# Where the ends of the expert rows, the copies of the partial sums and the first expert's steps stand in the queues of a fused mixer and mixture-of-experts kernel

## The reference

```python
x = L0_attn_x
xn = _layernorm(x)
# mixer: projection to 2*1024, causal depthwise convolution (4 taps), silu,
# a scan over time with 64 states, gate, projection back to 512, layernorm
attn = _layernorm(W_out(y * silu(x_gate)) + xn, ln_gamma, ln_beta)
# experts: 8 of them, each takes the 1024 rows with its highest scores
scores = (tanh(xn @ gate_w.T) + 1) * 0.5
vals, idx = top_k(scores.T, 1024)
y = _layernorm(xn[idx], ln_gamma, ln_beta)
h = gelu(y @ fc1s[e].T + b1s[e])          # 512 -> 2048
o = (h @ fc2s[e].T + b2s[e]) * kept_w     # 2048 -> 512
ffn = xn.at[idx].add(o)
return x + attn + ffn
```

## Time and profile before

| | us |
|---|---|
| median of three runs | 2714.39 |
| time of the profiled execution | 2714.52 |
| span of the profiled execution | 2712.8 |
| TensorE (matmul) busy in it | 2643.2 |
| VectorE busy | 2061.1 |
| ScalarE busy | 1484.9 |
| GpSimd busy | 685.4 |
| mean granted share of TensorE's clock | 0.996 |

### The profile page before, as it was taken

How to read it: one execution, slowest core, us unless ns; L and a number is a source line. 1 busy time by engine, 2 the same in 40 slices (tenths; PEclk the granted TensorE clock), 3 DMA queues, 4 the chain that set the end, 5 groups by cost and what they waited for, 6 DMA issues and landing times.

```text
span 2712.8 us, 41479 instructions
## 1 busy us (share of the span) xinstructions
PE 2643.2 (97%) x11818; PEld 2137.0 (79%) x11820; DVE 2061.1 (76%) x3533; ACT 1484.9 (55%) x2569; POOL 685.4 (25%) x1002
## 2 busy tenths in 40 slices
PE   8999999999999999999999999999999999999997
PEld 4588888888887788888778777887878778788886
DVE  8778888888788888888865867877678676786654
ACT  5744455555555555665445555565555555555552
POOL 5422222222221222224330313122141121411102
PEclk9999999999999999999999999999999999999999
DMA  9633323222333333224442425234262342533413
GB/s 365 248 124 109 108 79 95 90 92 95 96 105 109 109 109 109 78 93 124 151 129 93 121 71 137 78 91 116 70 147 70 94 125 67 131 87 89 102 47 70
DMA packets 139517, 299.99 MB, mean 111 GB/s; under 512 B 26080, under 2 KB 26208, under 8 KB 135520
## 3 DMA queue, kind: packets, MB, share of 16 engines
q1 hardware_dynamic: 105696, 201.54, 22.4%
q0 software_dynamic: 33664, 96.75, 14.9%
HBM read 244.46 MB, written 53.77 MB: 110 GB/s over the span
## 4 chain that ended last, share of the span: by engine, by line
PE 86%; DVE 6%; issue 4%; ACT 2%; DMA 1%; POOL 0%; DVEq 0%; SPq 0%; ACTq 0%; POOLq 0%
PE ring L1546 8%; PE ring L1547 8%; PE ring L1548 8%; PE po L2451 7%; PE po L2453 7%; PE po L2452 7%; PE pb L2451 4%; PE pb L2453 4%; PE pb L2452 4%; PE po L1584 4%; PE po L1585 4%; PE po L1586 4%; PE pc L2453 2%; PE pc L2451 2%; PE pc L2452 2%
## 5 line engine op out<-in xcount | busy, mean ns | idle before, releaser
L2451 PE MATMUL po<-w2h,hid_h 128*128 128x512 f32 x1024 | 404.9, 395 | 18.2 <-DVE res L2310 12.9
L2452 PE MATMUL po<-w2l,hid_h 128*128 128x512 f32 x1024 | 400.3, 391 | 0.0
L1546 PE MATMUL ring<-xt_h,w_h 128*128 128x512 f32 x1024 | 400.1, 391 | 0.1
L1547 PE MATMUL ring<-xt_l,w_h 128*128 128x512 f32 x1024 | 398.5, 389 | 0.0
L1548 PE MATMUL ring<-xt_h,w_l 128*128 128x512 f32 x1024 | 398.4, 389 | 0.0
L1339 DVE SCALAR_TENSOR_TENSOR u<-xin,cw,u 128x512 f32<-128x512 f32 x384 | 288.5, 751 | 74.2 <-issue 32.8
L2451 PEld LDWEIGHTS po<-w2h,hid_h 128*128 128x128 f32 x1024 | 193.4, 189 | 62.9 <-DVE res L2310 14.2
L1961 POOL DMA_INDIRECT out_dram<-res,idx_c x64 | 114.6, 1791 | 504.9 <-DVE res L2310 492.4
L1546 PEld LDWEIGHTS ring<-xt_h,w_h 128*128 128x128 f32 x1024 | 192.2, 188 | 41.0 <-DVE xt_l L542 0.9
L2452 PEld LDWEIGHTS po<-w2l,hid_h 128*128 128x128 f32 x1024 | 193.4, 189 | 38.7
L1548 PEld LDWEIGHTS ring<-xt_h,w_l 128*128 128x128 f32 x1024 | 192.2, 188 | 40.1
(11 more groups left out here) (294 smaller groups left out, 6255.5 us busy)
## 6 DMA issues: line engine op xcount, KB each, us to landing
w2r<-fc_in SPq DMA_DIRECT2D x256, 256.0 KB
wo<-wo_halves POOLq DMA_DIRECT2D x120, 512.0 KB, 4.2
w1r<-fc_in SPq DMA_DIRECT2D x144, 256.0 KB
x_tail<-x_in SPq DMA_DIRECT2D x64, 256.0 KB, 2.7
out_dram<-res SPq DMA_DIRECT2D x64, 256.0 KB, 2.0
g_x<-x_in SPq DMA_DIRECT2D x15, 1024.0 KB, 8.5
xt_rows<-g_xnt SPq DMA_DIRECT2D x15, 1024.0 KB, 10.2
rows<-xt_rows SPq DMA_DIRECT2D x15, 1024.0 KB, 6.2
```

The lines of the kernel that those rows point to most:

```text
L1546: pe.matmul(ring[r % 2][:, :], w_h[:, r, q], xt_h[:, k, :], start=(k == 0), stop=False)
L1547: pe.matmul(ring[r % 2][:, :], w_h[:, r, q], xt_l[:, k, :], start=False, stop=False)
L2451: pe.matmul(dst, ah, bh, start=start, stop=False, skip_group_check=more)
L2452: pe.matmul(dst, ah, bl, start=False, stop=False, skip_group_check=more)
```

## The change

It moves instructions and waits; no arithmetic is added but one ScalarE activation of a single column.

- **Row ends.** `rows_out` becomes `row_out`, one bank at a time. In the last pair (q = 7) the four row ends of the first half stand between the low parts of tiles 18 to 21 and of weights 16 and 17, and the first steps on the next expert's transposed rows (`T_HIGH_AT[0]`, `T_LOW_AT[0]`) stand there too.
- **Partial sums.** In every pair ScalarE copies `top` out of R0 before the gelu of `first`, not behind it.
- **Passage.** The gate activation 7 of the mixer's last block stands ahead of the second `y_high` copy; ScalarE's four `sum_rows` of that block move into the first four steps of expert 0; a one-column gelu stands ahead of the expert's first; VectorE makes the low part of the second weights later than the first weights'; each gelu waits for one bank's `take` and not for all four.
- **Expert 0.** GpSimd gathers expert 0's second rows first, then adds the mixer's beta, then gathers expert 1's first rows, and then takes the square roots for expert 0's second rows. The steps of VectorE, ScalarE and TensorE on rows stand at other step numbers (`ROWS_1_AT`, `ROWS_2_AT`, `TAIL_AT`, `BIAS_AT`, `T_AT`, `FIRST_..._AT`).
- **The end.** In expert 7 the last three tiles are shared bank by bank, not the last two.

```diff
--- before.py
+++ after.py
@@ -1280,10 +1280,13 @@
                 w_high(3)
             in_g(b, 6)
             side(1)
+            if last:
+                in_g(b, 7)
             y_high(b, 2)
             if first_turn:
                 w_high(4)
-            in_g(b, 7)
+            if not last:
+                in_g(b, 7)
             side(2)
             y_high(b, 3)
             side(3)
@@ -1301,11 +1304,8 @@
                 if last and k >= 2:
                     sums.first_high(act, k - 2)
                 ends.normal_rows(act, b, k)
-                if last and k >= 1:
-                    ends.sum_rows(act, b, k - 1)
             if last:
                 group_high(KD - 1)
-                ends.sum_rows(act, b, J - 1)
 
         act.wait_ge(sums.c_small_in, 16 * 8 + 1)
...
@@ -1721,7 +1721,7 @@
 LOWS = ("B11", "T1", "B22", "T3", "B21", "T2", "T4")
 BANKS = ("B11", "B12", "B22", "B21")
 P1, P2, P6, P5, P7, P4, P3 = range(1, 8)
...
@@ -1734,7 +1734,9 @@
 
 
     G = 2 * E
-    T_AT = (8, 9, 11, 12)
+    T_AT = (9, 10, 12, 13)
...
@@ -1972,16 +1978,15 @@
 
         pool.wait_ge(sums.c_t, KD + 1)
         pool.wait_ge(sums.c_in_all, NB * NW + 1)
+        take(idx_c[1][:, :], 1, 1)
+        pool.wait_ge(c_kp, 1 + 1)
+        gather(rows[1], idx_c[1], lambda j: c_ga[1])
         for j in range(J):
             ends.add_beta(pool, NB - 1, j)
         ends.inverse_std(pool, NB - 1)
-        take(idx_c[1][:, :], 1, 1)
-        pool.wait_ge(c_kp, 1 + 1)
-        gather(rows[1], idx_c[1], lambda j: c_ga[j])
+        next_rows(1, 0, 2)
         inverse_std(1)
-        gather_gates(ew.row_gates, idx_c[1], lambda j: c_ga[j])
-        pool.wait_ge(c_kp, 2 + 1)
-        next_rows(1, 0, 2)
+        gather_gates(ew.row_gates, idx_c[1], lambda j: c_ga[3])
         inverse_std(2)
         pool.wait_ge(c_t, 2 * KD + 1)
         next_rows(1, 1, 3)
...
@@ -2035,10 +2042,14 @@
         w_high(act, s, s)
 
     def first_low(dve, s):
-        if s == 1:
+        if s == 0:
+            w1_low(dve, 0)
+        else:
             dve.wait_ge(c_bias, 16 + 1)
             bias(dve, 0, 1)
-        w_low(dve, s, s)
+            w2_low_of(dve, 0)
+            w1_low(dve, 1)
+            w2_low_of(dve, 1)
 
...
@@ -2119,12 +2130,12 @@
             w2_high(e, 2 * q)
             if q < PAIRS - 1:
                 a_high(e, q + 1, here + P2)
+            act.wait_ge(c_p1, here + P6 + 1)
+            act.wait_ge(c_p2, shared(e, FT + 2 * q) - 128 + 1)
+            act.copy(top, R0[:, :]).then_inc(c_ge, 1)
             act.wait_ge(c_b1, e + 1 + 1)
             act.wait_ge(c_add, adds(e, q, ADD_FIRST) + 1)
             gelu(first, first, 2 * q).then_inc(c_ge, 1)
-            act.wait_ge(c_p1, here + P6 + 1)
-            act.wait_ge(c_p2, shared(e, FT + 2 * q) - 128 + 1)
-            act.copy(top, R0[:, :]).then_inc(c_ge, 1)
             act.wait_ge(c_ge, steps(e, q, TOP_LEFT) + 1)
             hid_high(e, 2 * q, first)
...
             if q == PAIRS - 1:
-                for x in (2, 3, 4, 5):
-                    store_high(e, x)
-                for x in (FT, FT + 1):
-                    w2_high(e, x)
+                store_high(e, 2)
+                w2_high(e, FT)
+                store_high(e, 3)
+                w2_high(e, FT + 1)
+                store_high(e, 4)
+                if not last:
+                    for k, name in T_HIGH_AT[0]:
+                        t_high(e + 1, k, name, here + P3)
+                store_high(e, 5)
...
-        act.wait_ge(ends.c_po, NB * J + 1)
+        act.wait_ge(c_b1, 1 + 1)
+        act.activation(warm, ends.half[:, 0:1], ACT.Gelu_apprx_tanh)
         for n in range(2 * FT):
             g, s = n // FT, n % FT
             raw_l = old_w(n)
+            if n < J:
+                act.wait_ge(ends.c_po, (NB - 1) * J + n + 1 + 1)
             act.wait_ge(c_p2, shared(0, n - 4) + 1 if n >= 4 else 1)
             if n >= 12:
                 act.wait_ge(ends.c_fin, NB * J + 1)
@@ -2186,6 +2205,8 @@
             act.copy(old_h(n)[:, :], raw_l).then_inc(c_hh, 1)
             if n + 2 < 2 * FT:
                 next_high(n + 2)
+            if n < J:
+                ends.sum_rows(act, NB - 1, n)
             if g == 0 and s - 1 in T_AT:
                 row_high(T_AT.index(s - 1))
             if g == 1:
...
+            elif s in TAIL_AT:
+                ends.scale(dve, NB - 1, TAIL_AT.index(s))
+                ends.finish(dve, NB - 1, TAIL_AT.index(s))
...
@@ -2302,13 +2323,12 @@
             dve.wait_ge(c_sc[j], 16 * g)
             dve.tensor_scalar(res[j][:, :], b2[:, :], kept[i][:, j, bass.ds(e, 1)], None, ALU.mult).then_inc(c_bw, 1)
 
-        def rows_out(e, i):
+        def row_out(e, i, j, count=2):
             g = 2 * e + i
             dve.wait_ge(c_bw, (g + 1) * J + 1)
-            for j in range(J):
-                dve.wait_ge(c_p2, 128 * e + J * (i * FT + FT - 2) + 2 * (j + 1) + 1)
-                dve.scalar_tensor_tensor(out=res[j][:, :], in0=po[j][:, :], scalar=kept[i][:, j, bass.ds(e, 1)],
-                                         in1=res[j][:, :], op0=ALU.mult, op1=ALU.add).then_inc(c_rw, 1)
+            dve.wait_ge(c_p2, 128 * e + J * (i * FT + FT - count) + count * (j + 1) + 1)
+            dve.scalar_tensor_tensor(out=res[j][:, :], in0=po[j][:, :], scalar=kept[i][:, j, bass.ds(e, 1)],
+                                     in1=res[j][:, :], op0=ALU.mult, op1=ALU.add).then_inc(c_rw, 1)
 
         def pair(e, q, last):
             first, low, top = hid_w[2 * q % 4], store_w[2 * q + 1], store_w[2 * q]
...
             if q == PAIRS - 1:
-                for x in (2, 3, 4, 5):
-                    hid_low(e, FT + x)
-                for x in (FT, FT + 1):
-                    w2_low(e, x)
+                hid_low(e, FT + 2)
+                w2_low(e, FT)
+                row_out(e, 0, 0)
+                hid_low(e, FT + 3)
+                w2_low(e, FT + 1)
+                row_out(e, 0, 1)
+                hid_low(e, FT + 4)
+                if not last:
+                    for step in T_LOW_AT[0]:
+                        t_step(e + 1, step, here + P3)
+                row_out(e, 0, 2)
+                hid_low(e, FT + 5)
+                row_out(e, 0, 3)
 
...
-            if g == 0 and 3 <= s < 3 + J:
-                ew.statistics(dve, 1, s - 3, rows[1])
-            if g == 0 and s >= FT - J:
-                row_statistics(1, 0, s - FT + J)
+            if g == 0 and s in ROWS_1_AT:
+                row_statistics(0, 1, ROWS_1_AT.index(s))
+            if g == 0 and s in ROWS_2_AT:
+                row_statistics(1, 0, ROWS_2_AT.index(s))
             if g == 1 and s < J:
                 row_statistics(1, 1, s)
             if n + 2 < 2 * FT:
-                w_low(dve, n + 2, n + 2)
+                w1_low(dve, n + 2)
+                w2_low_of(dve, n + 2)
             if g == 0:
                 tail(s)
-            if g == 0 and 3 <= s < 3 + J:
-                ew.normalise(dve, 1, s - 3, rows[1])
-            if g == 0 and s >= FT - J:
-                row_normalise(1, 0, s - FT + J)
+            if g == 0 and s in ROWS_1_AT:
+                row_normalise(0, 1, ROWS_1_AT.index(s))
+            if g == 0 and s in ROWS_2_AT:
+                row_normalise(1, 0, ROWS_2_AT.index(s))
...
@@ -2434,7 +2464,8 @@
                     w1_low_c(1, 0)
                     w1_low_b(1, 0)
             if n == FT - 1:
-                rows_out(0, 0)
+                for j in range(J):
...
@@ -2497,12 +2529,13 @@
             three(po[j][:, :], h[:, w], l[:, w], w2h[x % 4][:, :], w2l[x % 4][:, :], start, stop).then_inc(c_p2, 1)
 
         def old_share(n):
+            pe.wait_ge(c_wl, 2 * n + 2 + 1)
             pe.wait_ge(c_hl, n + 1 + 1)
             if n == 0:
                 pe.wait_ge(ends.c_po, NB * J + 1)
-            if n == FT:
-                pe.wait_ge(c_rw, J + 1)
             for j in range(J):
+                if n == FT:
+                    pe.wait_ge(c_rw, j + 1 + 1)
                 share(j, old_h(n), old_l(n), n, n % FT == 0)
 
         def tile(e, x):
@@ -2519,20 +2552,18 @@
                     pe.wait_ge(c_rw, (2 * e + x // FT - 1) * J + j + 1 + 1)
                 share(j, h, l, x, x % FT == 0)
 
-        def last_shares(e, x):
-            pe.wait_ge(c_hl, halved(e, x) + 1)
-            pe.wait_ge(c_wl, w2_at(e, x) + 1)
+        def last_shares(e, *tiles):
             for j in range(J):
-                h, l = tile(e, x)
-                share(j, h, l, x)
-                if j == 0:
-                    pe.wait_ge(c_hl, halved(e, x + 1) + 1)
-                    pe.wait_ge(c_wl, w2_at(e, x + 1) + 1)
-                h, l = tile(e, x + 1)
-                share(j, h, l, x + 1, False, True)
+                for x in tiles:
+                    if j == 0:
+                        pe.wait_ge(c_hl, halved(e, x) + 1)
+                        pe.wait_ge(c_wl, w2_at(e, x) + 1)
+                    h, l = tile(e, x)
```

(12 more changed lines are left out.)

74 lines of the change are left out of this document (42 added, 32 removed).

## The result

The changed kernel takes 2700.14 us (median of 5, 2697.94 to 2701.75) against 2714.31 (median of 5, 2713.46 to 2715.4). The ratio is 0.9947, 95% interval 0.9934 to 0.9961: 14.2 us faster. Its profiled execution took 2700.72, with a span of 2699.0. The page gives TensorE 2647.5 us busy; before had 2643.2, and the arithmetic is the same, so part of what is saved in waits has come back as slower matmuls.

A forecast was written before the change was run, and what follows sets the result against it. TensorE, busy 2643.2 of 2712.8 us, was taken to bound the kernel. Terms -17.2 - 0.8 - 3.0 + 5.7 + 1.0 - 4.1 - 1.8 = -20.2 took 2714.5 to 2694.3, stated as 2694, range 2683 to 2703.

The forecast's parts named there:

- main case: Whole kernel: all terms hold as summed, 2694 us, own range 2689 to 2700; chance 62%.
- rival C: Loop edge only half cured, P4 or the last shares waiting for the late gelu: 2703 us; chance 10%.
- Loop edge: Start of experts 2 to 6: TensorE's waits on the copy of `top` go, with their clock loss; -17.2 us.
- D: All 56 pairs: the early copy delays ScalarE's high part of `first`, slower than before, 2728 us; chance 6%.
- Middles: Middle of experts 1 to 7: the last row end comes at the same time, so little is gained; -0.8 us.
- Rival B: Middles of experts: the row ends' waits go too, 2682 us; chance 10%.
- Stall in step 4: Expert 0: GpSimd's late root holds VectorE's low part of tile 4; TensorE idles +5.7 us, clock +1.0.
- VectorE's price for the four additions: Expert 0's steps: GpSimd's beta additions slow VectorE, 4.4 us if nothing hid them; nothing was added to the sum.
- A: Expert 0: no stall, additions and root run while VectorE has other work; 2687.6 us; chance 12%.
- Rest of expert 0: Expert 0 after the stall: waits where halves meet and near the end go, step 15's grows; -4.1 us.
- Passage: From mixer to expert 0: sums, table load and `w2l` leave the queues' way, shortening TensorE's waits; -3.0 us.
- The end: Expert 7's end: three tiles bank by bank let the last scatter start at 2699.2, not 2700.97; -1.8 us.

The follow-up runs named there:

- top_only: The kernel before with only the copy of `top` moved ahead of the gelu of `first` in every pair; 2706.26 us, ratio 0.9959.
- rows_early: The changed kernel with the first half's row ends moved earlier, ahead of low parts and T steps that TensorE wants later; 2680.95 us, ratio 0.9875.
- after_again: The changed kernel measured and profiled once more, with nothing changed; 2700.95 us.
- root_first: rows_early with the first square root of expert 0's second rows ahead of the gather of expert 1's rows on GpSimd; 2672.96 us, ratio 0.9849.
- rows_step4: rows_early with statistics and normalisation of expert 0's first group of second rows in step 4 instead of step 3; 2671.2 us, ratio 0.9842.

## Why the prediction was right, and where it was off

I forecast 2694 with 2683 to 2703 and got 2700.14: inside the range, 6 us slower than the point, and just outside the main case's own 2689 to 2700. In part that is luck: the range reached to 2703 for rival C, which didn't happen, and the slow stretches that used this room up were in no case of mine. The first 1200 us, which the change doesn't touch, gave 1.6 back by chance.

- **Loop edge, -17.2: right** (-17.5), in mechanism and size, the slow stretches included. top_only shows it alone. The path behind it was as named: the gelu is still late, and the last shares cover it. C and D are out: TensorE has no wait on sums, nor any in the 56 pairs.
- **Middles, -0.8: the step that failed.** The waits themselves are as worked out: 1.26 + 0.33 in two pieces with 2.13 lost, against 2.21, so -0.08 each for 0.1. The sign of the step is wrong for a reason that I had in hand. I priced slow stretches where they were to vanish and where the new stall was, and took it that the middles, with no such stretch in before, would have none after. With the edge's pauses gone, the middles' own pauses are followed by slow stretches, in four or five of six: +6.8, or 7.0 more than the term said. This is the larger part of what went wrong; step 4 and the rest of expert 0 add 2.4, and the first 1200 us and small spacings took some 3 off. A pause of 1.9 that cost 2.2 with its refill in the profile of before costs 3.8 in that of top_only; a price read from one trace of before didn't hold. Rival B's reading (waits gone) was no better; rows_early shows that it takes another order than the change's.
- **Stall in step 4, +5.7 and +1.0: right**, +7.5. The idle part was 4.89, since GpSimd's chain from the end of L176 to the root took 6.8 and not 7.9: the gathers took 0.95 to 1.07 each, and the earlier trace rows had 1.52 for the first. The clock's part was 2.3, not 1.0, and above the 1.9 that I had as its most: the clock was at 0.51 for 5.1 us, longer than in the stretch of the earlier trace rows. VectorE's price for the four additions, 4.4 at most, was 2.2: two of them made a `w2l` take 1.78 and 1.77, two met none, and TensorE waited for neither. A is out, and root_first and rows_step4 show both links.
- **Rest of expert 0, -4.1: mis-sized**, -2.5. The wait where the halves meet went, the two near the end went, and the one in step 15 grew to 1.94, one more than before's 0.90, as said. The missing 1.6 is one slow stretch behind it, which after_again doesn't have. Again a slow stretch that I had priced at nothing.
- **Passage, -3.0: right** as a sum (-2.9), less so in its parts. The view behind the earlier trace rows has eight kinds of waits and 36.0 us, not seven and 35.3: I left out the one on `sg`, 0.7, and with it a seventh wait of the passage. The early gate activation shortened it and made one on `u_l` in its place. Of the `u_l` waits only the last, 0.73, went; the others are about as long as before or longer. The 0.98 on `xt_l` and the 1.49 at the first share went whole. Of the change's parts the sums of rows give 1.0, the warm gelu 1.1, and the gate activation costs 0.4. The other 1.2 (the low part of the second weights made later, one bank's `take` for each gelu) weren't tried alone.
- **The end, -1.8: right**, -1.6.

What stays open is which moment makes the clock fall. The runs show that among pauses of 1.6 to 2.6 us it isn't the length (1.59 in two pieces, 1.9 and 2.6 all had both outcomes), nor their being split, nor the program. The same wait of 1.94 in step 15 stands in ten of the profiles, and three have a slow stretch behind it. Length does count further up: the wait of 4.9 in step 4 was followed by one in all eight profiles that have it. What comes before the pause and the moment at which it falls weren't separated.
